# Six sweeps over one matrix: a tile on chip serves two sweeps at once, chunk order alternates, and the tiles at the diagonal are held

## The chip, the core and the metric

The kernel runs on one core of a Trainium2 chip. The metric is the device time of one launch in microseconds (us). Before the change it is 1440.37 us, the median of 3 runs (1439.02 to 1440.63).

## The reference

A residual stack of four graph layers on x (4096 nodes, 128 features) and a dense fp32 matrix adj of 4096 x 4096 (64 MiB). Cut to what matters:

```python
x = layernorm(x + inv_deg * (adj @ x + beta * x) @ K + bias)                 # layer 0
h = relu(adj @ (x @ W1) + b1); h = relu(adj @ (h @ W2) + b2)                 # layer 1, width 20
x = layernorm(x + relu(relu(adj @ (h @ W3) + b3) + x))
x = layernorm(x + (adj * dinv[:, None] * dinv[None, :]) @ (x @ W + b))       # layer 2
x = layernorm(x + adj @ x + gamma * softmax(x Wl (x Wr).T) @ x @ Wh @ Wg)    # layer 3
```

adj is multiplied six times, each time with something that depends on the whole result of the time before: x (sweep 0), three times a matrix 20 wide (sweeps 1, 2, 3), the layer-2 features (sweep 4), x again (sweep 5). The attention at the end reads no adj.

## The kernel before

Everything is laid out transposed: a sweep makes 8 chunks of 512 output columns (the 512 rows of adj that belong to them), each the sum over 32 blocks of 128 source nodes. The adj tile `tile(c, g)` is 128 x 1024 fp32, 512 KB: two source blocks (2g, 2g+1) for chunk c. 16 tiles make a chunk. SyncE streams tiles into an 8-slot ring `raw` (`wait_slot` L258, the DMA L424), held back until the consumers of the tile 8 earlier are done.

- Sweep 0 (`first_sweep`, L1094): the stationary operand is a 128 x 128 block of x, the tile moves through TensorE in plain fp32. VectorE adds up the tiles for the row sums of adj (`row_sum`, L701 to 724). While it streams, 8 of the 32 blocks of each chunk are put into lasting buffers (`kept_t`, `kept_s`, `kept_v`, `resident`).
- Sweeps 1 to 3 (`narrow_sweep`, L1127): the stationary operand is a block of h, 20 columns wide. `add` (L1136) places the products of four successive blocks in four column groups of the array, `a[32 * j:...]`. The kept blocks (8, and with `kept_l` 9) come from SBUF, so 11.5 tiles of a chunk are streamed.
- Sweeps 4 and 5 (`wide_sweep`, L1185): split fp32r arithmetic. ScalarE makes `t_hi` (L589), VectorE `t_lo` (L829), TensorE three products per block. Sweep 4 streams 14 tiles a chunk and takes the last four blocks from `resident` in plain fp32 (L1227); sweep 5 streams 16.
- Each chunk has an epilogue, done during the next chunk on fixed places of each engine's program (`hooks`, L1143): the accumulator is copied to `at` (ScalarE, L534); `epilogue_1` multiplies by a small weight (for sweeps 1 and 2 `comb`, which adds the four column groups); sweeps 0, 3 and 4 then have residual and layer norm (VectorE L748 to 808, ScalarE `xn` L559), a transposition (`epilogue_3`, L1053) and a product (`epilogue_4`, L1069); sweeps 1 and 2 have a relu (L542) and `epilogue_2` (L1045). The last step writes 512 columns of the next sweep's operand: `next_h` (L576) or `laplacian_h` (L810).

All sweeps take the chunks in the order 0 to 7 and the source blocks 0 to 31, so the operand block that is finished last is needed last. Orders are written out by hand, the same on every engine; nothing is scheduled by a planner.

Of the kernel before, what the change touches and what calls it, by code (L numbers as in the profile page):

```python
# [3 lines left out]

# [3 lines left out]
F32 = mybir.dt.float32  # L8
# [56 lines left out]
def done(stage, s, c):  # L65

    return c + (1 + NC * sum(q < s for q in STAGES[stage]))


def build(nc, adj_s, x_dram, beta_in, ident_in, comb_in, w, out):  # L70
    with ExitStack() as ctx:
# [32 lines left out]
        with ExitStack() as narrow:  # L104
            kept_v = sb("kept_v", [P, NC * CW], F32, narrow)
# [5 lines left out]
        with ExitStack() as whole:  # L111
            resident = sb("resident", [P, RB, NC * CW], F32, whole)
# [58 lines left out]
        e2, e3 = e23[:, 0:CW], e23[:, CW:PW]  # L171
        free_banks = (e0, e1)
# [1187 lines left out]
```

## Time and profile before

| | us |
|---|---|
| median of 3 runs | 1440.37 |
| the profiled execution | 1445.9 |
| its span, first to last instruction | 1444.3 |
| TensorE busy in it | 1367.3 (95%) |
| VectorE busy | 899.6 (62%) |
| ScalarE busy | 709.5 (49%) |
| HBM read | 342.65 MB |

The mean granted clock of TensorE is 0.992. Busy times of matmuls have modelled ends, so a busy TensorE need not be a TensorE at its peak: sweeps with four products side by side and sweeps with one at a time both read as busy. The profile records every plain fp32 matmul as two instructions (two passes), a split fp32r one as one.

### The profile page before, as it was taken

How to read it: one execution, taken by the hardware profiler on the slowest of the kernel's cores; microseconds unless marked ns; L12 is line 12 of the kernel's file. 1: busy time of each engine (PE TensorE's matmuls, PEld its weight loads, DVE VectorE, ACT ScalarE, POOL GpSimd, SP SyncE). 2: the span in 40 equal slices, each digit the busy share in tenths (PEclk: the TensorE clock that was granted, in tenths of full speed). 3: DMA queues.
4: the chain of work that ended last, by engine and by line, in shares of the span. 5: the costliest groups of instructions: out<-in, count | busy, mean ns of one | idle time of the engine just before them, and what ended most of it. 6: DMA issues, size and time to landing. Idle time of an engine off the chain costs nothing.

```text
span 1444.3 us, 17225 instructions
## 1 busy us (share of the span) xinstructions
PE 1367.3 (95%) x5879; PEld 798.7 (55%) x5879; DVE 899.6 (62%) x1194; ACT 709.5 (49%) x883; POOL 254.9 (18%) x167
## 2 busy tenths in 40 slices
PE   6999999888898999999999999999899999999987
PEld 2555555321222222247777778888667777767754
DVE  4676777300000013368888898888788888888885
ACT  1110011111101111257777787776787887887786
POOL 0111111000000000101010000000533333345345
PEclk9999999999999999999999999999999999999999
DMA  9866677699999999998999999997000000000000
GB/s 361 332 260 233 253 277 271 248 391 406 407 404 408 408 401 408 390 362 301 313 323 309 338 324 365 354 386 271 0 0 1 0 1 0 1 1 29 0 1 29
DMA packets 103455, 345.69 MB, mean 239 GB/s; under 512 B 11610, under 2 KB 13274, under 8 KB 103386
## 3 DMA queue, kind: packets, MB, share of 16 engines
q1 hardware_dynamic: 101136, 343.98, 63.3%
q10 hardware_dynamic: 2250, 0.82, 0.2%
q8 instruction: 41, 0.67, 0.2%
q14 instruction: 28, 0.23, 0.0%
HBM read 342.65 MB, written 2.10 MB: 239 GB/s over the span
## 4 chain that ended last, share of the span: by engine, by line
PE 75%; DMA 15%; DVE 5%; ACT 3%; issue 1%; POOL 0%; SPq 0%; DVEq 0%; ACTq 0%
DMA raw<-in_adj_s 15%; PE acc L1104 11%; PE acc L1140 9%; PE acc L1202 7%; PE acc L1197 7%; PE acc L1198 7%; PE acc L1297 6%; PE acc L1124 4%; PE acc L1227 2%; PE acc L1287 2%; PE acc L1291 2%; PE acc L1288 2%; DVE t_lo L829 2%; PE e L1252 2%; PE e L1254 2%; PE e L1253 2%
## 5 line engine op out<-in xcount | busy, mean ns | idle before, releaser
L829 DVE TENSOR_TENSOR t_lo<-raw,t_hi 128x1024 fp32r<-128x1024 f32 x240 | 292.1, 1248 | 42.4 <-ACT t_hi L589 36.9
L589 ACT ACTIVATE t_hi<-raw 128x1024 fp32r<-128x1024 f32 x240 | 251.5, 1058 | 60.4 <-PE acc L1202 58.9
L1197 PE MATMUL acc<-t_hi,st_hi 128*128 128x512 f32 x480 | 202.3, 421 | 2.9 <-DVE st_lo L734 2.9
L500 POOL TENSOR_TENSOR ring_lo<-ring,p_hi 128x1024 fp32r<-128x1024 f32 x64 | 155.6, 2430 | 220.2 <-ACT p_hi L647 220.1
L1198 PE MATMUL acc<-t_hi,st_lo 128*128 128x512 f32 x480 | 187.5, 391 | 0.0
L1140 PE MATMUL acc<-raw,h_a 128*20 128x512 f32 x736 | 161.8, 599 | 25.8 <-DMA raw<-in_adj_s 25.5
L1104 PE MATMUL acc<-raw,x 128*128 128x512 f32 x384 | 174.0, 608 | 11.2 <-DMA raw<-in_adj_s 11.2
L760 DVE TENSOR_TENSOR xs<-e,bias 128x512 f32<-128x512 f32 x8 | 5.5, 690 | 272.0 <-PE e L1020 272.0
L534 ACT ACTIVATE at<-acc 128x512 f32<-128x512 f32 x48 | 28.7, 598 | 266.4 <-PE acc L1140 181.9
L913 DVE TENSOR_TENSOR ring<-ring,e 128x1024 f32<-128x1024 f32 x128 | 154.1, 1212 | 0.7 <-PE e L1267 0.6
L1202 PE MATMUL acc<-t_lo,st_hi 128*128 128x512 f32 x480 | 149.9, 393 | 0.7 <-DVE t_lo L829 0.7
L641 ACT ACTIVATE ring<-ring 128x1024 f32<-128x1024 f32 x128 | 134.3, 1054 | 25.0 <-DVE ring L913 24.9
L472 POOL COPY x<-xn 128x512 f32<-128x512 f32 (+1 forms) x24 | 20.4, 851 | 672.6 <-ACT xn L559 672.6
L1104 PEld LDWEIGHTS acc<-raw,x 128*128 128x128 f32 x384 | 73.6, 195 | 99.0 <-issue 99.0
L1297 PE MATMUL acc<-ring,x 128*128 128x512 f32 x256 | 120.9, 595 | 0.0
L724 DVE TENSOR_TENSOR rsum<-rsum,raw 128x1024 f32<-128x1024 f32 x80 | 105.6, 1320 | 17.0 <-DMA raw<-in_adj_s 11.6
L1197 PEld LDWEIGHTS acc<-t_hi,st_hi 128*128 128x128 f32 x480 | 90.2, 188 | 31.1 <-issue 8.1
L1198 PEld LDWEIGHTS acc<-t_hi,st_lo 128*128 128x128 f32 x480 | 90.3, 188 | 24.6 <-issue 7.2
L1202 PEld LDWEIGHTS acc<-t_lo,st_hi 128*128 128x128 f32 x480 | 88.8, 188 | 23.8 <-DVE t_lo L829 5.6
L1140 PEld LDWEIGHTS acc<-raw,h_a 128*20 128x20 f32 x736 | 24.4, 98 | 130.8 <-DMA raw<-in_adj_s 100.2
L1140 PE MATMUL acc<-raw,rsum 128*20 128x512 f32 x368 | 84.0, 598 | 11.8 <-DMA raw<-in_adj_s 11.7
L891 DVE TENSOR_TENSOR peak<-e,peak 128x1024 f32<-128x1024 f32 x54 | 66.1, 1224 | 41.0 <-ACT ring L653 40.9
(189 smaller groups left out, 2062.1 us busy)
## 6 DMA issues: line engine op xcount, KB each, us to landing
raw<-in_adj_s SPq DMA_DIRECT2D x600, 512.0 KB, 6.9
resident<-in_adj_s SPq DMA_DIRECT2D x16, 512.0 KB, 7.7
raw<-in_adj_s SPq DMA_DIRECT2D x24, 256.0 KB, 7.7
kept_t<-in_adj_s SPq DMA_DIRECT2D x8, 512.0 KB, 5.8
x<-in_x SPq DMA_DIRECT2D x4, 512.0 KB, 8.4
kept_s<-in_adj_s SPq DMA_DIRECT2D x8, 256.0 KB, 6.1
kept_v<-in_adj_s SPq DMA_DIRECT2D x8, 256.0 KB, 6.5
kept_l<-in_adj_s SPq DMA_DIRECT2D x8, 256.0 KB, 9.0
```

Of the source, the lines that this page charges most:

```text
L500: nc.gpsimd.tensor_tensor(ring_lo[:, n % RING, :], slot(n), p_hi[:, m % 2, :].bitcast(F32), ALU.subtract).then_inc(pl_done, 1)
L589: nc.scalar.activation(t_hi[:, (par * wide_tiles(s) + g) % HL, :], raw[:, k, :], ACT.Copy).then_inc(hi_done, 1)
L641: nc.scalar.activation(slot(n), slot(n), ACT.Exp).then_inc(exped, 1)
L724: nc.vector.tensor_tensor(mine, mine, other, ALU.add).then_inc(sum_done, 1)
L829: nc.vector.tensor_tensor(t_lo[:, k, :], raw[:, slot_no(s, c, g), :], t_hi[:, k, :].bitcast(F32), ALU.subtract).then_inc(lo_done, 1)
L913: nc.vector.tensor_tensor(part, part, row, ALU.subtract).then_inc(subbed, 1)
L1104: i = mm(a[:, :], block_of(x0, g * GB + j), raw[:, k, j * CW:(j + 1) * CW], start=(g == 0 and j == 0), stop=False)
L1140: return mm(a[32 * j:32 * j + H, :], h[:, b * H:(b + 1) * H], moving, start=(n < 4), stop=(n >= NB - 4))
L1197: mm(a[:, :], block_of(st_hi, b), hi[:, m], start=(b == 0), stop=False)
L1198: mm(a[:, :], block_of(st_lo, b), hi[:, m], start=False, stop=False)
L1202: i = mm(a[:, :], block_of(st_hi, b), lo[:, m], start=False, stop=(b == NB - 1))
L1297: r = mm(o, block_of(x, b), slot(n)[:, u * CW:(u + 1) * CW], start=(b == 0), stop=(b == NB - 1))
```

## The change

1. **Two sweeps per tile.** In sweeps 0, 1 and 2, a tile (c, d), with d the group of 512 source nodes, is also multiplied by the next sweep's operand for d, when that is finished already: `joined(s, c, d)`, true if d stands at least AHEAD[s] = 1, 2, 2 places before c in the order of the sweep. The product goes to a bank of its own (`ahead`, the halves of `rs01`), ScalarE copies it to `sums` (`store_ahead`), and the next sweep does not use that tile: `used`. Its copy to `at` adds `sums` and moves to VectorE (`evacuate_narrow`).
2. **The order alternates.** `ORDER`: sweeps 0 and 2 take chunks 0 to 7, sweeps 1 and 3 take 7 to 0.
3. **The tiles at the diagonal are held.** For each c the 4 tiles of two d (c and c+1; 6 and 7 for chunk 7) have their own 16 KB and stay from sweep 0 to sweep 3 (chunk 1's from the start of sweep 1, `load_late`), in place of one strip for all chunks. The kept tiles come last in a chunk.
4. **What follows from it.** Ring positions are now counted by a list of items (`ITEMS`). Sweep 4 has nothing held and streams all 16 tiles, its first chunk in reverse; most of its stationary operand is made during sweep 3, a chunk at a time (`st_hi`, `st_lo` 512 columns wide). Hooks in sweep 3 are spread by `TURNED`. In sweeps 1 to 3 the first chunk waits for the epilogue of the last chunk of the sweep before (`hooks(-1)`) before its own first tile.

Tiles by chunk, in each sweep's own order of chunks (an item is one tile of 512 KB used by one chunk, held or streamed):

| sweep | items per chunk | streamed per chunk | items for two sweeps |
|---|---|---|---|
| 0 | 16 each | 12 each (chunk 1: 16), and 4 x 7 into held buffers | 0, 2, 4, 6, 8, 10, 12, 14 |
| 1 | 2, 4, 6, 8, 10, 12, 14, 16 | 0, 0, 2, 4, 6, 8, 10, 12 (and 4 late) | 0, 0, 2, 4, 6, 8, 10, 12 |
| 2 | 4, 6, 8, 10, 12, 14, 16, 16 | 0, 2, 4, 6, 8, 10, 12, 12 | 0, 0, 2, 4, 6, 8, 10, 12 |
| 3 | 4, 6, 8, 10, 12, 14, 16, 16 | 0, 2, 4, 6, 8, 10, 12, 12 | none |

```diff
+ORDER = (tuple(range(NC)), tuple(reversed(range(NC))), tuple(range(NC)), tuple(reversed(range(NC))))
+AHEAD = (1, 2, 2)
+KEPT = tuple((c, c + 1) if c + 1 < NC else (c, c - 1) for c in range(NC))
+def joined(s, c, d):
+    return s < len(AHEAD) and used(s, c, d) and ORDER[s].index(c) - ORDER[s].index(d) >= AHEAD[s]
+def used(s, c, d):
+    return s == 0 or not joined(s - 1, c, d)
...
+        ahead = [rs01[:, 0:CW], rs01[:, CW:PW]]
...
+            def evacuate_narrow(s, r):
+                ...
+                dve.wait_ge(pe_acc, s * NC + r + 1)
+                dve.wait_ge(S["mm1"], done("mm1", s, r) - 1)
+                if stored(s - 1, c):
+                    dve.wait_ge(sums_done, stored(s - 1, c))
+                    nc.vector.tensor_tensor(at[:, :], acc[r % 2], sums[:, c, :], ALU.add).then_inc(S["at"], 1)
+                else:
+                    nc.vector.tensor_copy(at[:, :], acc[r % 2]).then_inc(S["at"], 1)
...
+                for n, i in enumerate(items):
+                    ...
+                    for j in range(GB):
+                        b, k = i.d * CB + i.h * GB + j, 32 * (2 * i.h + j)
+                        m = mm(a[k:k + H, :], h[:, b * H:(b + 1) * H], t[:, j * CW:(j + 1) * CW],
+                               start=(i.d == items[0].d), stop=(i.d == items[-1].d))
+                    if i.fused:
+                        for j in range(GB):
+                            b, k = i.d * CB + i.h * GB + j, 32 * (2 * (1 - i.h) + j)
+                            m = mm(f[k:k + H, :], h_next[:, b * H:(b + 1) * H], t[:, j * CW:(j + 1) * CW],
+                                   start=(i.d == joint[0]), stop=(i.d == joint[-1]))
...
-                    if s == S5:
-                        continue
-                    if g in KEPT_AFTER and not first(c):
-                        kept = [KEPT_AFTER.index(g)]
...
-                        i = mm(a[:, :], block_of(source(s), NS * GB + j), resident_of(c, j, j + 1)[:, 0, :],
-                               start=False, stop=(j == RB - 1))
```

How the instructions move. First TensorE in sweep 0, the second half of chunk 3 and the start of chunk 4, after the change. `rs` is the bank for the products put aside, `e` a bank for epilogues, `acc` the sweep's own sum.

```order
L1256 MATMUL acc<-raw,x 128x512 x8
L1203 MATMUL e<-ident,xn 128x128 x4
L1256 MATMUL acc<-kept_t,x 128x512 x4
L1219 MATMUL e<-w,xt 128x20 x4
L1256 MATMUL acc<-kept_t,x 128x512 x4
L1256 MATMUL acc<-raw,x 128x512 x4
L1264 MATMUL rs<-raw,h_a 20x512 x4
L1283 MATMUL acc<-ident,bx 128x128 x4
L1256 MATMUL acc<-raw,x 128x512 x4
L1264 MATMUL rs<-raw,h_a 20x512 x4
```

Behind each four wide products of a joined d stand four narrow ones, a set, that were not there. Next TensorE in an early chunk of a narrow sweep. Before, all of them look like this (sweep 1):

```order
L1017 MATMUL e<-at,comb 128x512
L1140 MATMUL acc<-raw,h_a 20x512 x4
L1045 MATMUL e<-w,xt 128x20 x4
L1140 MATMUL acc<-raw,h_a 20x512 x17
L1140 MATMUL acc<-kept_l,h_a 20x512
```

Now, the end of sweep 0 and the first two chunks and a half of sweep 1:

```order
L1283 MATMUL acc<-ident,bx 128x128 x4
L1163 MATMUL e<-k,at 128x128 x4
L1165 MATMUL e<-ones_f,rsum 128x1 x4
L1203 MATMUL e<-ident,xn 128x128 x4
L1219 MATMUL e<-w,xt 128x20 x4
L1324 MATMUL acc<-kept_v,h_a 20x512 x4
L1324 MATMUL acc<-kept_s,h_a 20x512 x4
L1167 MATMUL e<-at,comb 128x512
L1324 MATMUL acc<-kept_s,h_a 20x512 x4
L1195 MATMUL e<-w,xt 128x20 x4
L1324 MATMUL acc<-raw,h_a 20x512 x2
L1329 MATMUL rs<-raw,rsum 20x512 x2
```

The whole epilogue of sweep 0's last chunk now stands in a row with no tile work between its steps, and the first chunks are a few products long. Last, VectorE in sweep 3 after the change, one chunk (here the third):

```order
L855 TENSOR_TENSOR at<-acc,sums 128x512
L882 TENSOR_TENSOR xs<-e,bias 128x512
L886 SCALAR_TENSOR_TENSOR xs<-xs,xb 128x512
L898 SCALAR_TENSOR_TENSOR xs<-xs,xb 128x512
L913 BN_STATS stats<-xs 128x6 x4
L918 BN_AGGR mv<-stats 128x2 x4
L921 TENSOR_SCALAR ve<-mv 128x4
L927 RECIPROCAL rstd<-std 128x4
L929 SCALAR_TENSOR_TENSOR nmr<-mv,rstd 128x4
L936 TENSOR_TENSOR v<-e,bias_l 128x512
L938 TENSOR_TENSOR v<-v,dinv 128x512
L843 TENSOR_TENSOR st_lo<-v,st_hi 128x512
```

The copy to `at` and the making of `st_lo` are new in this queue; before, sweep 3 had only the nine rows from `xs` to `v` there.

## Rows read from the trace of the kernel before

**Rows 1.** The page: TensorE busy tenths and HBM traffic in 40 equal slices
```profile
PE   6999999888898999999999999999899999999987
GB/s 361 332 260 233 253 277 271 248 391 406 407 404 408 408 401 408 390 362 301 313 323 309 338 324 365 354 386 271 0 0 1 0 1 0 1 1 29 0 1 29
```
**Rows 2.** Windows by stage: length, busy us by engine, clock, DMA share, GB/s
```profile
44.80:265.10 220.30, 220.30 (x702) 112.54 (x703) 162.17 (x238) 25.51 (x64) 29.53 (x21) 1.00 0.70 263
265.10:391.90 126.80, 109.60 (x611) 27.40 (x610) 3.56 (x17) 14.05 (x30) 1.23 (x2) 0.97 0.96 376
391.90:510.70 118.80, 106.98 (x592) 28.01 (x592) 0.00 (x0) 12.11 (x24) 0.00 (x0) 1.00 1.03 407
510.70:632.40 121.70, 112.52 (x662) 34.62 (x662) 35.95 (x112) 24.57 (x56) 8.63 (x14) 1.00 1.02 401
632.40:663.40 31.00, 28.42 (x114) 18.67 (x114) 30.32 (x48) 21.78 (x35) 2.18 (x2) 1.00 0.88 303
663.40:825.40 162.00, 162.00 (x673) 123.68 (x673) 137.52 (x192) 118.24 (x143) 14.79 (x14) 1.00 0.92 317
...
1011.30:1444.30 433.00, 409.16 (x1623) 287.99 (x1621) 346.60 (x406) 343.23 (x364) 184.65 (x99) 0.99 0.01 6
```
**Rows 3.** TensorE in order of time, sweeps 1 and 2: start, length, what
```profile
290.50 2.77 PE L1140 MATMUL acc<-raw,h_a 128*20 128x512 f32 x24
299.84 1.12 PE L1017 MATMUL e<-at,comb 128*128 128x512 f32 x2
300.89 1.09 PE L1140 MATMUL acc<-raw,h_a 128*20 128x512 f32 x8
301.91 1.06 PE L1045 MATMUL e<-w,xt 20*128 20x20 f32 x8
302.90 1.64 PE L1140 MATMUL acc<-raw,h_a 128*20 128x512 f32 x8
304.78 1.04 PE L1140 MATMUL acc<-raw,h_a 128*20 128x512 f32 x4 [0.24 <-DMA raw<-in_adj_s]
```
**Rows 4.** ScalarE in order of time, sweep 1: relu and the copy of h
```profile
301.00 0.68 ACT L542 ACTIVATE xt<-e,b 20x512 f32<-20x512 f32 x1 [2.14 <-PE e L1017]
303.01 0.24 ACT L576 ACTIVATE rsum<-e 128x80 f32<-128x80 f32 x1 [1.33 <-PE e L1045]
```
**Rows 5.** TensorE in order of time, chunk 0, and the last weights' user on GpSimd
```profile
27.88 9.13 PE L1104 MATMUL acc<-raw,x 128*128 128x512 f32 x16 [5.17 <-DMA raw<-in_adj_s]
39.05 1.37 POOL L467 TENSOR_TENSOR bx<-x,beta 128x512 f32<-128x512 f32 x1 [38.60 <-DMA beta<-in_beta]
```
**Rows 6.** ScalarE in order of time: ends of chunks 0 and 7 of sweep 0, the norm behind
```profile
44.81 0.60 ACT L534 ACTIVATE at<-acc 128x512 f32<-128x512 f32 x1 [12.41 <-PE acc L1124]
265.17 0.60 ACT L534 ACTIVATE at<-acc 128x512 f32<-128x512 f32 x1 [7.61 <-PE acc L1124]
272.48 1.65 ACT L559 ACTIVATE xn<-xs,nmr,rstd 128x128 f32<-128x128 f32 x4 [0.44 <-DVE nmr L807]
```
**Rows 7.** Windows of 3 us behind sweep 0: clock is third from the right
```profile
275.00:278.00 3.00, 0.81 (x5) 0.04 (x2) 0.00 (x0) 0.47 (x1) 0.62 (x1) 0.95 1.00 395
278.00:281.00 3.00, 3.00 (x8) 1.32 (x8) 0.00 (x0) 0.00 (x0) 0.00 (x0) 0.50 1.03 423
```
**Rows 8.** VectorE in order of time, sweep 3, one epilogue
```profile
544.94 0.69 DVE L760 TENSOR_TENSOR xs<-e,bias 128x512 f32<-128x512 f32 x1 [2.37 <-PE e L1020]
549.22 0.16 DVE L807 SCALAR_TENSOR_TENSOR nmr<-mv,rstd 128x4 f32<-128x4 f32 x1
```
**Rows 9.** Groups of instructions in 663.4:825.4 (sweep 4 without its first chunk)
```profile
L829 DVE TENSOR_TENSOR t_lo<-raw,t_hi 128x1024 fp32r<-128x1024 f32 x98 | 119.7, 1251 | 23.3 <-ACT t_hi L589 22.5
L1227 PE MATMUL acc<-resident,v 128*128 (+1 forms) x56 | 28.5, 590 | 0.0
```
**Rows 10.** TensorE in order of time, two tiles of sweep 4 begin
```profile
710.90 0.39 PE L1197 MATMUL acc<-t_hi,st_hi 128*128 128x512 f32 x1
712.27 0.60 PE L1029 MATMUL e<-ident,at 128*128 128x128 f32 x4
```

More of the change, by code:

```diff
@@ L423, in step @@
+            first_of_1 = min(i.seq for r in range(NC) for i in ITEMS[1, r] if not i.kept)
+            def step(s, c, par):
+                if s in FLAT:
+                    flat(s, c)
+                    return
+                for g in range(NG):
+                    wait_slot(sp, s, c, g)
                     k = slot_no(s, c, g)
-                    sp.dma_start(raw[:, k, :n], tile(c, g)[:, :n]).then_inc(raw_in[k], 16)
+                    sp.dma_start(raw[:, k, :], tile(c, group_no(s, c, g))).then_inc(raw_in[k], 16)
@@ L534, in evacuate, with store_ahead @@
                 nc.scalar.activation(at[:, :], acc[par][:, :], ACT.Copy).then_inc(S["at"], 1)
+            def store_ahead(s, r):
+                if (s, r) not in STORES:
+                    return
+                act.wait_ge(pe_acc, s * NC + r + 1)
+                if s > 0:
+                    act.wait_ge(S["at"], done("at", s, r))
+                nc.scalar.activation(sums[:, row(s, r), :], ahead[r % 2], ACT.Copy).then_inc(sums_done, 1)
             def second(s, c):
@@ L602, in step @@
-                if has_before:
-                    next_h(ps, pc)
+                early = 3 if s == S4 and first(c) else 0
+                for g in range(NG):
+                    if s == S4 and first(c) and g in S4_PREPARED:
+                        stationary_hi(S4, S4_PREPARED[g])
+                    if s == S5 and first(c) and g % 2 == 0:
+                        stationary_hi(S5, g // 2)
+                    k = slot_no(s, c, g)
+                    act.wait_ge(raw_in[k], landed(s, c, g))
+                    if not (s == S4 and first(c) and g < HL):
+                        act.wait_ge(pe_tile, tile_no(s, c, g) - (HL - 1))
+                    nc.scalar.activation(t_hi[:, g % HL, :], raw[:, k, :], ACT.Copy).then_inc(hi_done, 1)
+                    if g == 2:
+                        evacuate(ps, pc, 1 - par)
+                    if g == 4:
+                        second(ps, pc)
+                    if g == 8 - early:
+                        deviation(ps, pc)
+                    if g == 10 - early:
+                        normalise(ps, pc)
+                    if g == 12 - early:
+                        transposed(ps, pc)
```

597 lines of the change are left out of this document (326 added, 271 removed).

## The prediction

> **What bounds the kernel now.** I read the 40 slices first, then the windows by stage, then each stage in order of time. TensorE reads as 95% busy throughout, but the traffic says more: about 400 GB/s from 265 to 632 us, 230 to 320 in most other stages with tiles, none in the last 433 us [rows 1, 2]. So there are two regimes.
>
> Sweep 0 is TensorE's: seven chunks take 220.3 us, 31.5 each, without a gap, at 263 GB/s [rows 2]. Sweeps 1 to 3 take 367.3 us and are bound by the stream: 407 GB/s is 1.29 us per 512 KB tile, and 12 tiles (11.5, and half a late one) or 11.5 of them make the 15 us of a chunk. TensorE waits there a little before every tile (the last row of the group) [rows 3]. Sweep 4 is again TensorE's (162 of 162 us, 23.1 a chunk), VectorE close behind with 137.5 [rows 2]. The attention reads no tile of adj; the change leaves its instructions alone, I cost it at nothing.
>
> What a tile costs TensorE differs by a factor of four. A narrow product is recorded twice; 24 records are 12 products, and they take 2.57 us without the drain of the last (2.77 with it) [rows 3]: 0.86 us for a set of four in four column groups. A wide one takes 0.86 alone (427 ns per record).
>
> **Sweep 0.** Added: a set of four narrow products for each joined d, 7+6+...+1 = 28 sets. Nothing covers them, since TensorE is full. Floor 0.86 each; with a change to another shape and back, 1.05: a single `comb` product, worth 0.86, takes 299.84 to 300.89 [rows 3]. 28 x 1.0 = **+28**. ScalarE's and VectorE's share (copies of 0.6 us) hides beside 32 us chunks. In chunk 0 the kept tiles no longer stand ahead of streamed ones, so the hole of 5.17 us [rows 5] should close, and the slow-clock work behind it, some 2 us. Against it: the small weights are issued behind x, whose last quarter now comes six transfers later (8 us); `bx` waited for them until 38.6, and the chunk ended at 44.8 [rows 5, 6]. Bounds: -7 and +3; I take **-3**, since the queue is emptier when the weights come. Sweep 0 ends at 265.1 + 25 = 290.
>
> On the changes of shape, the Trainium skill, "TensorEngine Tiling (Array Packing)", Key Properties, says that changing the tiling mode drains TensorE. By that rule the higher price stands for each of the 28; row and rule agree, and the sum with the floor would be 4 us lower.
>
> **Sweeps 1 to 3, the stream.** It falls from 280 tile loads to 42+4, 54 and 54: 154 x 1.29 = 198 us. If the stream still set the end, 169 us would go. I think it does not, for three reasons.
>
> *Products.* Sweep 1 has 144 own and 84 joint products, 57 sets, 49 us; sweep 2 has 172+84, 64 sets, 55 us; sweep 3 172, 43 sets, 37 us. The epilogue's two steps take 1.05 + 0.99 [rows 3]: 14.4 for seven chunks in sweeps 1 and 2. So sweep 1 needs 63.4 of TensorE against 59 of stream of which 8 tiles are in the ring already; sweep 2 69.4 against 69.4, again less 8 tiles. The short chunks come first and read held tiles, so the ring is full when the long ones begin (two tiles of ring remain at the end of sweep 2 by my count). Both are TensorE's by a hair; I add 1 us for stalls.
>
> *Entries.* Before, the chunk finished last was needed last. Now the first chunk of each sweep needs it at once. Behind sweep 0 that is: accumulator to the start of `xn` 7.3, `xn` 1.65 [rows 6], transposition 0.75, copy 0.6, product 1.0, copy 0.3 = **11.8**, nothing beside it on TensorE. Behind sweeps 1 and 2: copy 0.9 on VectorE, `comb` to relu 1.2, relu to the next step 0.9, that 1.1, copy of h 0.3 [rows 3, 4] = **4.4** each.
>
> *The chain in sweep 3.* VectorE's queue is now strictly one chunk after the other. From the copy to `at`: 2.1 to the first `xs` (copy, then `epilogue_1`), 4.3 to `nmr` [rows 8], then ScalarE's norm 1.65, `st_hi` 0.75, and `st_lo` 0.8, the two steps to `v` fitting in between: 10.0 us a round, 6.6 and 8 for the first two without `st_lo`. Followed through chunk by chunk, two accumulators deep, the chunks take 1.7, 3.7, 8.9, 8.6, 11.0, 13.9, 14.7, 13.6: the last three also wait in TensorE's program for the norm and its two products. That is 76, against 61 of TensorE's work and 59 of stream. With the entry, 80.5.
>
> *The clock.* Behind sweep 0 TensorE was busy 0.8 of 3 us; then the granted clock was 0.50 (1.2 of 2.4 GHz) [rows 7]. The new entries and the early chunks of sweep 3 idle for 2 to 5 us at a time. I charge 4 us at sweep 1 (6.5 us of work at half speed, part of it waits), and 4.5 in sweep 3, where products in the chain double. The Trainium skill, "TensorE: Matmul & The Clock Gate", Part 1, calls the throttled clock the default, which activity releases; by that rule, as by the row, the idle entries are paid for again in the products behind them. With a clock that stays up the sum would be 8.5 lower.
>
> Sweep 1: 11.8 + 63.4 + 0.8 + 4 = 80. Sweep 2: 4.4 + 69.4 + 1 = 75. Sweep 3: 85. Together 240, was 367.3: **-127**.
>
> **Sweep 4.** Per chunk, the four plain products of held blocks go (8 records, at least 3.4 us) and two split tiles come. One tile is 1.37 us [rows 10], so 16 x 1.37 + 0.36 for the transposition = 22.2 against 23.1. VectorE: 119.7/98 = 1.22 per tile [rows 9]; 19.6 a chunk less 14 of them leaves 2.55, plus 16 is 22.1; stream 16 x 1.29 = 20.6. Three near-equals jostle; I take 22.7: 7 x -0.43 = **-3**. The first chunk loses eight halves of operand making on VectorE but gets the norm epilogue and two tiles more, 29.5 instead of 31: **-1.5**. Sweep 5 keeps its work: 0.
>
> **Sum.** +25 - 127 - 4.5 = -106.5. The profiled execution is 1445.9 with a span of 1444.3; the median lies 5.5 below the profiled one, and I apply the difference to the median: 1440.4 - 106.5 = 1334.
>
> **Rivals.**
>
> 1. *Everything quicker.* The clock stays up (in the attention TensorE idles in small pieces, busy 409 of 433 us, at a clock of 0.99 [rows 2]), sets cost the floor in sweep 0, weights land early: 1334 - 8.5 - 4 - 3 = 1318.
> 2. *The ring is too shallow.* Eight slots must hide a landing time that was long only because the queue was full; but when TensorE frees slots in bursts, tiles come late in the long chunks. If each of the 80 tiles of the long chunks (22, 34 and 24 in the three sweeps) costs 0.4 us, 1334 + 32 = 1366. For it: sweep 2 ends with two tiles of ring to spare. Against it: sweeps 1 to 3 before held 401 to 407 GB/s with the same ring [rows 2].
> 3. *Two banks do not mix.* The rows show four groups at once within one bank and with four moving tiles. A joint item has two products for `acc` and two for `rs`. If the two pairs run one after the other, the 84 joint items of sweeps 1 and 2 cost 0.86 more, on the engine that sets the end: 1334 + 72 = 1406.
> 4. *Slower.* The same place, without any overlap in a joint item: four products in a row are 3.44 us instead of 0.86. The 84 items cost +217, and the 28 sets of sweep 0 +72: 1623. It decides from 0.95 us per set upwards (106.5 over 112 sets). Against it: groups overlapped for different tiles and different weights; only the bank is new.
> 5. *The change does not do what it says.* The table of items and the rows of the order leave no room for that: the streamed tiles of sweeps 1 to 3 are 150 and four late ones.
>
> **Chances.** Forecast 0.63, rival 1 0.13, rival 2 0.12, rival 3 0.07, rival 4 0.04, unforeseen 0.01. The forecast's own range is 1324 to 1350: the unknown of chunk 0 (-4, +6), of the clock (-5, +10). With rivals 1 and 2 it becomes 1314 to 1368, which leaves out a little over one in ten. About 0.2% (3 us) is what a measurement tells from no change. All cases but the fourth lie far below the time before; one in a hundred is for a mixture near it. Faster 0.94, same 0.01, slower 0.05.
>
> **What would show it.** Right: sweep 0 ends near 290, each chunk about 1 us longer than the last; `acc` and `rs` narrow products start together, eight records per 0.86 us; sweeps 1 and 2 show traffic of 300 GB/s, not 407, and TensorE full in their long chunks; gaps of 11 and twice 4 us between sweeps; in sweep 3 VectorE's queue is a closed chain and TensorE waits for `at` and `xn`, with clock below 1.0; sweep 4's chunks take 22 to 23 us. Wrong: joint items of 1.7 us or more; waits for `raw` in sweeps 1 and 2 summing to more than 10 us; a clock of 0.5 through whole sweeps; a sweep 4 chunk above 23.5, which would mean that VectorE or ScalarE sets it.

## The result and the profile after

The changed kernel takes 1360.42 us (median of 4 runs, 1359.1 to 1362.38) against 1440.5 for the kernel before: a ratio of 0.9447, 95% interval 0.943 to 0.9463. The prediction was 1334 in a range of 1314 to 1368. The sign and the mechanism were right; the gain is 80 us and not 106.5.

The page of the changed kernel, TensorE and the traffic in 40 slices, and what was read:

```profile
PE   8799999998999988899999999999899999999987
GB/s 374 203 338 247 234 224 207 205 203 131 369 302 377 359 285 407 300 358 374 375 380 376 333 356 360 385 355 0 1 1 0 1 1 1 0 18 15 0 1 31
HBM read 284.98 MB, written 2.10 MB: 212 GB/s over the span
```

Against [rows 1] the long stretch at 400 GB/s has gone; between slices 11 and 17 the traffic swings from 285 to 407. The windows by stage (chunk 0; the rest of sweep 0; sweeps 1, 2, 3; the first chunk of sweep 4, its other seven; sweep 5; attention), columns as in [rows 2]:

```profile
0.00:46.30 46.30, 31.45 (x73) 14.79 (x74) 20.21 (x19) 5.18 (x5) 2.47 (x6) 0.94 0.88 335
46.30:300.10 253.80, 253.80 (x925) 114.41 (x923) 161.19 (x231) 28.43 (x70) 29.13 (x21) 1.00 0.61 232
300.10:382.40 82.30, 73.75 (x555) 26.04 (x554) 8.39 (x25) 12.73 (x29) 1.22 (x2) 0.92 0.72 269
382.40:463.20 80.80, 78.31 (x592) 24.47 (x592) 5.54 (x9) 10.18 (x22) 0.00 (x0) 1.00 0.91 351
463.20:547.50 84.30, 75.66 (x494) 28.54 (x494) 44.39 (x125) 22.93 (x53) 9.08 (x14) 0.96 0.89 338
547.50:581.70 34.20, 27.92 (x119) 19.53 (x118) 27.92 (x39) 20.69 (x26) 1.23 (x2) 1.00 0.78 281
581.70:737.70 156.00, 156.00 (x701) 128.64 (x700) 150.89 (x204) 129.54 (x156) 15.93 (x14) 1.00 0.99 375
737.70:924.60 186.90, 185.31 (x839) 150.60 (x838) 165.80 (x160) 144.03 (x156) 11.83 (x9) 1.00 0.91 343
924.60:1357.30 432.70, 409.04 (x1622) 288.13 (x1620) 345.55 (x406) 342.80 (x364) 184.38 (x99) 0.99 0.01 6
```

Sweeps 1 to 3 went from 367.3 us [rows 2] to 247.4, with the clock at 0.92 to 1.00. Sweep 0 pays 35 for it. Each stage beside its forecast:

| stage | before | forecast | after | miss |
|---|---|---|---|---|
| chunk 0 of sweep 0 | 44.8 | 41.8 | 46.3 | +4.5 |
| rest of sweep 0 | 220.3 | 248.3 | 253.8 | +5.5 |
| sweep 1 | 126.8 | 80 | 82.3 | +2.3 |
| sweep 2 | 118.8 | 75 | 80.8 | +5.8 |
| sweep 3 | 121.7 | 85 | 84.3 | -0.7 |
| sweep 4, first chunk | 31.0 | 29.5 | 34.2 | +4.7 |
| sweep 4, seven chunks | 162.0 | 159 | 156.0 | -3.0 |
| sweep 5 | 185.9 | 185.9 | 186.9 | +1.0 |

With rounding these make the 19.5 us by which the spans' difference (1444.3 - 1357.3 = 87.0) falls short of 106.5. The remaining 7 of the 106.5 - 80 lie between span and median: the profiled execution of before lay 5.5 above its median, that of the change lies 1.3 below.

The chunk lengths below are differences between the starts of the copies of `acc` to `at`, one per chunk; they repeat from kernel to kernel to 0.05 us where the stream and the clock stay out of it. So the small edits are read from them; the medians of single edits of 3 us and less hardly stand out. (Sweep 3's last chunk ends here at its copy, 551.25 us in the changed kernel; the windows above end it at the first product of sweep 4, 547.5.) Chunk s.r is the r-th that sweep s works on (r from 0). Here the lengths in sweeps 0 to 3, and under them those of kernels of the experiments:

```
            0.0   .1   .2   .3   .4   .5   .6   .7 | 1.0   .1   .2   .3   .4   .5   .6   .7
changed    46.4 33.1 33.8 35.0 36.2 37.4 38.5 39.7 |14.9  3.8  8.2  8.3  9.2 10.9 12.6 14.3
before     44.8 31.5 31.5 31.5 31.5 31.5 31.5 31.5 |20.7 12.4 15.7 15.4 15.4 15.4 15.4 16.3
no joint   45.1 32.3 31.5 31.5 31.5 31.5 31.5 31.5 |25.9 17.0 15.3 15.4 15.3 15.4 15.3 15.3
all six    36.8 32.7 33.9 34.7 35.9 36.7 37.9 38.8 |12.7  4.5  6.3  8.6  9.2 10.9 12.6 14.3

            2.0   .1   .2   .3   .4   .5   .6   .7 | 3.0   .1   .2   .3   .4   .5   .6   .7
changed     5.6  5.7  7.4  9.2 10.1 12.1 15.3 15.4 | 7.2  6.4  8.8  9.3  9.3 15.3 13.9 17.8
before     16.5 13.2 14.7 14.7 15.3 14.8 14.7 14.8 |16.5 14.9 14.9 14.9 15.5 15.1 15.2 16.8
no joint   18.9 14.1 15.4 15.4 15.4 15.4 16.2 15.4 |16.9 16.9 15.3 15.4 15.3 16.7 15.3 18.8
no joint 2  5.6  5.7  6.6  7.4  8.3 12.5 15.3 15.3 |15.9 16.3 15.4 15.3 15.3 16.7 15.4 18.8
all six     5.6  3.8  8.3  8.3 10.0 11.8 15.7 15.4 | 5.6  6.3  8.3  7.6  8.3 16.0 14.2 19.0
```

### The profile page after: what moved, and what is told of

Its sections match the earlier page's. It is cut to its first block, busy times and chain, and to the rows that moved or that the text cites. A ratio compares the mean times of both kernels' runs of the same rounds, so it can differ in the third digit from the quotient of the medians.

```text
span 1357.3 us, 17259 instructions
## 1 busy us (share of the span) xinstructions
PE 1291.2 (95%) x5911; PEld 795.1 (59%) x5911; DVE 929.9 (69%) x1213; ACT 716.5 (53%) x880; POOL 255.3 (19%) x167
## 3 DMA queue, kind: packets, MB, share of 16 engines
HBM read 284.98 MB, written 2.10 MB: 212 GB/s over the span
## 4 chain that ended last, share of the span: by engine, by line
PE 69%; DVE 13%; issue 6%; ACT 5%; DMA 3%; ACTq 1%; SPq 1%; POOL 1%; DVEq 0%; POOLq 0%
PE acc L1256 14%; PE acc L1324 8%; PE acc L1445 7%; DVE t_lo L989 7%; PE acc L1363 4%; PE acc L1358 4%; PE acc L1359 4%; DMA raw<-in_adj_s 2%; PE rs L1264 2%; PE acc L1435 2%; PE acc L1436 2%; PE acc L1439 2%; PE rs L1329 2%; PE e L1400 2%; PE e L1402 2%
## 5 line engine op out<-in xcount | busy, mean ns | idle before, releaser
L989 DVE TENSOR_TENSOR t_lo<-raw,t_hi 128x1024 fp32r<-128x1024 f32 x256 | 307.4, 1243 | 23.9 <-ACT t_hi L711 18.9
L711 ACT ACTIVATE t_hi<-raw 128x1024 fp32r<-128x1024 f32 x256 | 262.8, 1055 | 39.5 <-PE acc L1363 37.8
L1359 PE MATMUL acc<-t_hi,st_lo 128*128 128x512 f32 x512 | 199.6, 390 | 0.0
L584 POOL TENSOR_TENSOR ring_lo<-ring,p_hi 128x1024 fp32r<-128x1024 f32 x64 | 155.4, 2428 | 220.4 <-ACT p_hi L765 220.3
L1363 PE MATMUL acc<-t_lo,st_hi 128*128 128x512 f32 x512 | 159.9, 393 | 5.3 <-DVE t_lo L989 5.0
L1358 PEld LDWEIGHTS acc<-t_hi,st_hi 128*128 128x128 f32 x512 | 96.2, 188 | 25.5 <-issue 3.1
L1359 PEld LDWEIGHTS acc<-t_hi,st_lo 128*128 128x128 f32 x512 | 96.2, 188 | 19.5 <-issue 0.2
L1041 DVE TENSOR_TENSOR peak<-rs,peak 128x1024 f32<-128x1024 f32 x61 | 74.5, 1221 | 25.5 <-ACT ring L771 25.3
L855 DVE TENSOR_TENSOR at<-acc,sums 128x512 f32<-128x512 f32 x19 | 13.1, 689 | 109.4 <-PE acc L1324 109.4
L771 ACT ACTIVATE ring<-rs 128x1024 f32<-128x1024 f32 x62 | 63.3, 1021 | 37.5 <-PE rs L1402 37.4
L1324 PE MATMUL acc<-raw,h_a 128*20 128x512 f32 x384 | 80.7, 600 | 2.1 <-DMA raw<-in_adj_s 1.4
L1400 PE MATMUL e<-q_hi,k_hi 128*128 128x512 f32 x122 | 69.6, 571 | 3.6 <-DVE peak L1041 1.8
```

The source lines that it names most:

```text
L584: nc.gpsimd.tensor_tensor(ring_lo[:, n % RING, :], slot(n), p_hi[:, m % 2, :].bitcast(F32), ALU.subtract).then_inc(pl_done, 1)
L711: nc.scalar.activation(t_hi[:, g % HL, :], raw[:, k, :], ACT.Copy).then_inc(hi_done, 1)
L989: nc.vector.tensor_tensor(t_lo[:, k, :], raw[:, slot_no(s, c, g), :], t_hi[:, k, :].bitcast(F32), ALU.subtract).then_inc(lo_done, 1)
L1041: nc.vector.tensor_tensor(peak[:, :], score_bank(t)[:, :], peak[:, :], ALU.max).then_inc(s_maxed, 1)
L1324: m = mm(a[k:k + H, :], h[:, b * H:(b + 1) * H], t[:, j * CW:(j + 1) * CW], start=(i.d == items[0].d), stop=(i.d == items[-1].d))
L1358: mm(a[:, :], block_of(st_hi, b), hi[:, m], start=(g == 0 and j == 0), stop=False)
```

## The experiments

**Where the gain comes from: joint tiles off.** All edits are made to the changed kernel.

```
-AHEAD = (1, 2, 2)
+AHEAD = (99, 99, 99)
```

> Edit to the changed kernel: no tile serves two sweeps (AHEAD = 99, 99, 99); the order of chunks still alternates and the tiles at the diagonal are still the ones held. Theory (the whole gain is the tiles that are not streamed a second time; the alternating order and the other choice of held tiles are worth nothing by themselves): sweep 0 gets 33 us shorter than in the changed kernel, sweeps 1 to 3 take 120 to 126 us each, the whole 1436 to 1448 us, within 0.5% of the kernel before. Rival (the order and the held tiles bring part of the gain): below 1430.

Measured: 1464.54 us, ratio 1.0154 (1.0136 to 1.0171). Both theories fell: without the joint tiles the rest of the change is a loss of 22 us. One window holds all of sweep 2:

```profile
401.10:527.10 126.00, 111.80 (x592) 27.42 (x592) 5.54 (x8) 7.33 (x16) 0.00 (x0) 0.97 1.01 400
```

The stream is as full as before [rows 2], and the products are the same 592, but 126.0 us in place of 118.8. The new layout holds 4 tiles of a row on chip, the old one 4.5 (blocks 23 to 31), so a full row streams 12 tiles and not 11.5: a chunk in the middle of sweep 2 takes 15.36 us, before 14.74. By the copies of `acc`, sweeps 1 to 3 lose 22.2 us and sweep 0 loses 1.0, while sweep 4, which holds nothing now, wins 4.4; that is 18.8 in all, less than the medians' 22, since the profiled execution of before lay above its median. Three sweeps stream 12 tiles more; at 1.28 us each they are worth 15 of those 22.2. The excess shows most in the first two chunks of a sweep (42.9 against 33.1 in sweep 1, 33.0 against 29.8 in sweep 2), where the program now puts the epilogue of the last chunk ahead of every product: in sweep 1 TensorE waits 6.20 us for `xn`, where before it worked through 16 products of the new sweep. Alternating order and held tiles were not tried apart from each other, so how the loss divides between them is not shown. The joint tiles bring 104 us (1464.5 to 1360.4); 80 is what is left when the order and the storage that they need are paid.

**Joint tiles off in one sweep.**

```
-AHEAD = (1, 2, 2)
+AHEAD = (99, 2, 2)
```

> Edit to the changed kernel: sweep 0 no longer puts products for sweep 1 aside (AHEAD = 99, 2, 2), so that sweep 1 reads all its tiles. Theory (a set put in between full-height products costs 1.18 us, 28 of them): sweep 0 behind chunk 0 takes 221 us in place of 253.9, sweep 1 is stream-bound at 12 x 1.285 = 15.4 us per chunk, 124 to 128 us in place of 82.3, the whole 1370 to 1376. Rival (sweep 0's extra time is in part its epilogues' new waits): sweep 0 behind chunk 0 stays above 228.

Measured: 1378.29 us (2 runs; 0.9558, 0.9538 to 0.9578). Sweep 0 behind chunk 0 takes 221.6 us against 253.85: 32.25 / 28 = 1.15 us per set, and the chunks of sweep 0 in the table grow by 1.18 from one to the next. The theory holds for sweep 0. Sweep 1 took 134.6, more than I expected, because the same two first chunks cost 42.4 here; the whole lies 2 us above my range for it.

```
-AHEAD = (1, 2, 2)
+AHEAD = (1, 2, 99)
```

> Edit to the changed kernel: sweep 2 no longer puts products for sweep 3 aside (AHEAD = 1, 2, 99), so that sweep 3 reads all its tiles. Theory (21 joint sets of 0.86 us go; where a chunk is bound by the stream they cost nothing): sweep 2 goes from 80.8 to 68 to 73 us, its last two chunks stay at 15.3 us, sweep 3 from 84.3 to 124 to 128 us, the whole 1388 to 1396. Rival (sets beside the others run at no cost, since they fill column groups that stood empty): sweep 2 stays above 78, the whole above 1398.

Measured: 1396.99 us (2 runs; 0.9688, 0.9668 to 0.9707). Sweep 2 took 76.8, between theory and rival. Chunks 2.2 and 2.3, with one and two sets less, are 0.86 and 1.72 us shorter; 2.4 is 1.76 shorter for three sets; 2.5 is 0.4 longer for four less, 2.6 and 2.7 unchanged. The whole is 1 us above my range. A joint set costs TensorE 0.86 in the early chunks and nothing in the late ones, where the stream sets the time:

```profile
383.67:424.00 40.33, 38.49 (x248) 13.10 (x248) 4.15 (x6) 5.97 (x13) 0.00 (x0) 1.00 0.87 325
424.00:460.50 36.50, 33.01 (x178) 7.46 (x176) 1.39 (x3) 1.83 (x4) 0.00 (x0) 1.00 1.03 410
```

In the changed kernel the last two chunks of sweep 2 run at the same rate, VectorE's copies of `acc` 15.3 us apart, which is 12 tiles:

```profile
432.48 0.69 DVE L855 TENSOR_TENSOR at<-acc,sums 128x512 f32<-128x512 f32 x1 [11.44 <-PE acc L1324]
447.82 0.69 DVE L857 COPY at<-acc 128x512 f32<-128x512 f32 x1 [14.65 <-PE acc L1324]
463.18 0.69 DVE L857 COPY at<-acc 128x512 f32<-128x512 f32 x1 [14.66 <-PE acc L1324]
```

**Chunk 0.** In the changed kernel TensorE (first row) and GpSimd (second) end it like this:

```profile
44.27 2.05 PE L1283 MATMUL acc<-ident,bx 128*128 128x128 f32 x8 [8.73 <-POOL bx L551]
...
43.08 1.04 POOL L551 TENSOR_TENSOR bx<-x,beta 128x512 f32<-128x512 f32 x1 [42.63 <-DMA beta<-in_beta]
```

`bx` waits for `beta`, the last constant, and starts 4.0 us later than before [rows 5], and TensorE stands for 8.7 us; then its clock is down (0.64 in 38 to 46 us) and the products behind take twice their time.

```
-            act.wait_ge(x_in[XP - 1], 16)
+            act.wait_ge(x_in[0], 16)
             for dst, src in consts:
```

> Edit to the changed kernel: ScalarE starts the DMAs of the constants when the first quarter of x has landed, not the last. Theory (chunk 0 waits for these loads: beta is the last of them and GpSimd's bx waits for it, TensorE then idles 8.7 us): the end of chunk 0 goes from 46.3 to 36 to 38 us, the whole to 1350 to 1352 us (-8 to -10). Rival (the loads take the queue time that tiles of row 0 need, so the tiles come later by as much): chunk 0 ends at 44 to 47 us, the whole stays within 2 us of 1360.

Measured: 1350.7 us (0.9369, 0.9344 to 0.9395), chunk 0 in 37.6. The same two instructions:

```profile
36.50 1.05 PE L1283 MATMUL acc<-ident,bx 128*128 128x128 f32 x8
...
32.34 1.12 POOL L551 TENSOR_TENSOR bx<-x,beta 128x512 f32<-128x512 f32 x1 [31.89 <-DMA beta<-in_beta]
```

The idle time is gone and the clock stays at 1.00 (2.4 GHz). The rival was right that the tiles come later: VectorE starts its ninth addition of a ring tile at 28.55 us, 25.81 in the changed kernel. But they are not late for TensorE, whose 48 records on ring tiles take 20.76 us in both kernels, without a wait. The theory holds.

**The sets of sweep 0.** One set between full-height products, in the changed kernel:

```profile
79.28 3.60 PE L1256 MATMUL acc<-raw,x 128*128 128x512 f32 x8
82.81 1.05 PE L1264 MATMUL rs<-raw,h_a 128*20 128x512 f32 x8
83.79 1.16 PE L1163 MATMUL e<-k,at 128*128 128x128 f32 x8
```

Eight full-height records are worth 8 x 0.427 = 3.42 us, but the set begins 3.53 us after them and takes 0.98 itself, not 0.86. The edit puts off the products of every first of two neighbouring source chunks and issues both sets behind the second:

```
+at = joint.index(i.d) // 2
+odd = at % 2 == 1
+alone_set = at >= (len(joint) // 2 - 1) // 2 * 2
-for b in range(CB):
+for back in ((2, 0) if odd and not alone_set else (0,) if alone_set else ()):
+    q = items[n - back].d
+    for b in range(CB):
...
-    elif i.h == 1:
+    elif i.h == 1 and alone_set:
         m.then_inc(pe_tile, 2)
+    elif i.h == 1 and odd:
+        m.then_inc(pe_tile, 4)
```

> Edit to the changed kernel: in sweep 0 the sets put aside for sweep 1 come in pairs, two sets of four products behind every second source chunk, where the source chunks stand next to each other (9 pairs of the 28 sets); the number of products is the same. Theory (a set costs 0.86 us for its products and 0.32 for the two changes between full-height products and column groups, together the measured 1.18): chunks 3 to 7 of sweep 0 get 0.32, 0.32, 0.64, 0.64 and 0.96 us shorter, the whole 2.9 us shorter, 1356.5 to 1358.5. Rival (1.18 us is what four such products take, whatever stands beside them): no chunk changes by over 0.1 us.

Measured: 1356.16 us (0.9418, 0.9404 to 0.9432). Chunks 3 to 7 are 0.33, 0.32, 0.66, 0.65 and 0.92 us shorter. A pair of sets is 16 records, and takes 1.85 us from its start to the start of what follows:

```profile
118.58 3.68 PE L1256 MATMUL acc<-raw,x 128*128 128x512 f32 x8
122.19 1.91 PE L1269 MATMUL rs<-raw,h_a 128*20 128x512 f32 x16
124.04 1.12 PE L1256 MATMUL acc<-raw,x 128*128 128x512 f32 x2
```

The eight records ahead take 3.61 of which 3.42 is theirs, the 16 take 1.85 of which 1.72: 0.32 for the change of shape and back, and 0.86 for each four products. The whole is 4.3 us shorter by the medians, more than the 2.9 of the chunks; single executions of it spread over 4.5 us.

**Half-filled sets.** TensorE in the changed kernel where chunk 2.3 begins; every product has two records, and `rs` is the bank for the next sweep:

```profile
400.09 0.60 PE L1324 MATMUL acc<-raw,rsum 128*20 128x512 f32 x2
400.50 0.60 PE L1324 MATMUL acc<-kept_e,rsum 128*20 128x512 f32 x2
400.52 0.60 PE L1324 MATMUL acc<-raw,rsum 128*20 128x512 f32 x2
400.94 1.05 PE L1329 MATMUL rs<-raw,h_a 128*20 128x512 f32 x8
401.79 1.03 PE L1324 MATMUL acc<-raw,rsum 128*20 128x512 f32 x4
402.75 1.13 PE L1167 MATMUL e<-at,comb 128*128 128x512 f32 x2
```

The two items have eight products in all, two full sets. But the `acc` products of the first half went ahead beside the chunk before, all four `rs` products follow at 400.94, and the `acc` products of the second half run alone at 401.79, two of them in the 0.86 us of four, since a full-height product comes next. An item with its h = 0 half directly ahead of an epilogue leaves such a hole. The edit moves the second epilogue behind an h = 1 half:

```
-if ps < 3 and (n == (min(4, len(items) - 1) if r > 0 else -1)):
+if ps < 3 and (n == (min(5, len(items) - 1) if r > 0 else -1)):
```

> Edit to the changed kernel: in sweeps 1 and 2 the second epilogue product of a chunk stands behind item 5 (behind both halves of a chunk's four blocks) and not behind item 4 (between the halves). Theory (a set of four row or column groups is left half filled where another shape comes between the halves, and the two halves then take 0.86 us each): chunks 2 and 3 of sweep 1 and chunks 1 to 3 of sweep 2 get 0.8 to 1.1 us shorter each, the whole 3.5 to 5 us shorter, 1355.5 to 1357. Rival (the extra microsecond is the wait for the epilogue's operand or the switch of shape itself): the chunks keep their lengths within 0.3 us, the whole within 1 us of 1360.

Measured: 1355.06 us (0.9398, 0.9377 to 0.942). In chunks of six items the epilogue now falls into the next one, so they are read in twos: 1.2 with 1.3 takes 14.87 us, was 16.50 (-1.63); 2.1 with 2.2 takes 12.06, was 13.14 (-1.08, where a new wait for `h_a` takes 0.48 of two sets); 2.3 is 0.84 shorter. Together that is 3.55 us, or 4.0 with the wait added back: five sets at 0.81. Of the whole's 5.4 another 1.5 lies in chunk 0, where `beta` landed earlier in that run; the rest is the balance of other chunks, chunk 3.0's 1.6 less at a clock of 1.00 among them. The theory holds.

**The entry of sweep 1.** TensorE's wait, and windows with the clock third from the right:

```profile
308.99 1.11 PE L1203 MATMUL e<-ident,xn 128*128 128x128 f32 x4 [6.19 <-ACT xn L652]
```
```profile
300.00:307.00 7.00, 2.11 (x18) 1.86 (x16) 3.33 (x16) 1.46 (x4) 0.00 (x0) 0.72 0.79 293
307.00:315.00 8.00, 4.91 (x24) 3.09 (x28) 0.22 (x2) 2.48 (x6) 1.22 (x2) 0.50 0.01 6
315.00:319.00 4.00, 4.00 (x24) 0.74 (x13) 0.82 (x2) 0.68 (x1) 0.00 (x0) 0.78 0.00 0
```

```
 epilogue_1(ps, pr, pr % 2)
+pe.wait_ge(sums_done, same_bank(1, 0))
+for b in [0, 1, 2, 3, 0, 1]:
+    mm(ahead[0], h_a[:, b * 128:b * 128 + 128], kept_x[:, 0, 0:CW], start=True, stop=True)
 epilogue_3(ps, pr)
```

> Edit to the changed kernel: six full-height products into a bank that nothing reads are put on TensorE between the epilogue products of sweep 0's last chunk, in the 6 us that it idles at the entry of sweep 1. They are extra work that no output uses. Theory (the idle time lowers the granted clock, 0.60 in 300 to 315 us and 0.78 in 315 to 319, and the products behind run at half speed): the granted clock from 307 to 319 us is above 0.9 and the sweep gets 2.5 to 4 us shorter, the whole 1356 to 1358. Rival (the entry is set by the chain of ScalarE and VectorE, not by products at a low clock): the clock rises and the time changes by under 1 us.

Measured: 1356.43 us (0.9418, 0.9393 to 0.9444). The windows of that kernel:

```profile
300.60:307.00 6.40, 5.72 (x25) 3.60 (x26) 3.18 (x15) 1.26 (x3) 0.00 (x0) 1.00 0.78 275
307.00:313.40 6.40, 4.36 (x28) 2.20 (x30) 0.42 (x4) 2.69 (x7) 1.23 (x2) 1.00 0.13 53
313.40:319.00 5.60, 5.09 (x38) 1.83 (x34) 1.34 (x2) 0.92 (x2) 0.00 (x0) 1.00 0.01 3
```

Chunks 1.0 and 1.1 take 12.74 + 2.92 us in place of 14.87 + 3.81: 3.0 us less. The clock of 0.5 (1.2 GHz) cost 3 us here, and the chain through ScalarE and VectorE the rest of the entry. The Trainium skill, "TensorE: Matmul & The Clock Gate", Part 1, says that activity releases the throttle; here products that nothing reads kept the granted clock at 1.00.

**Sweep 4's first chunk.**

```
ScalarE: deviation, normalise, transposed   g = 5, 7, 9  ->  6, 8, 12; st_hi(0) 13 -> 14
VectorE: residuals, statistics, scales      g = 2, 3, 4, 6  ->  3, 4, 5, 7; laplacian(0) 13, st_lo(0) 13 -> 14
TensorE: epilogue_3, epilogue_4             g = 8, 10  ->  9, 11
```

> Edit to the changed kernel: in the first chunk of sweep 4 the epilogue steps of sweep 3's last chunk and the preparation of stationary blocks 0 stand 1 to 3 groups later on ScalarE, VectorE and TensorE. Theory (that chunk takes 34.1 us against 22.3 for a later one partly because engines stand waiting, in program order, for epilogue steps that come too early): it becomes 28 to 31 us, the whole 3 to 6 us shorter. Rival (the chunk is bound by VectorE's work, 27.4 us busy, and by the clock): within 1.5 us of 34.1, the whole the same or up to 2 us longer.

Measured: 1358.18 us (0.941, 0.9389 to 0.9431). From the copy of `acc` at its start to the next one the chunk takes 28.0 us, was 30.46. Two waits of VectorE in the changed kernel:

```profile
554.77 0.69 DVE L882 TENSOR_TENSOR xs<-e,bias 128x512 f32<-128x512 f32 x1 [1.71 <-PE e L1170]
...
575.97 0.69 DVE L843 TENSOR_TENSOR st_lo<-v,st_hi 128x512 fp32r<-128x512 f32 x1 [0.70 <-ACT st_hi L607]
```

and the first of them with the later hooks:

```profile
558.37 0.69 DVE L882 TENSOR_TENSOR xs<-e,bias 128x512 f32<-128x512 f32 x1 [0.58 <-PE e L1171]
```

Hooks that came too early cost 2.5 us of the 4.7; my 3 to 6 was too much, and the rival's 1.5 too little.

**Four edits together.**

> The four edits together: constants asked for at the first quarter of x, second epilogue behind item 5, relaxed hooks in the first chunk of sweep 4, and six products that no output uses at the entry of sweep 1. Theory (they sit in different stretches and add up: 8.8 + 4.3 + 2.5 + 3 us by the traces of the single ones): 1340 to 1344 us, 0.930 to 0.933 of the kernel before. Rival (what is won ahead of a stretch that the stream bounds is lost in it): 1346 to 1352.

Measured: 1340.44 us, ratio 0.9292 (0.9276 to 0.9307). That is 18.9 us less than the changed kernel by the spans of the traces and 20.0 by the medians, where 18.6 was expected. They add up; the rival fell.

**Less stream in sweep 3, and what bounds its chunks.**

```
+near = 1 if s == 2 and c >= 3 else AHEAD[s] if s < len(AHEAD) else 0
-return s < len(AHEAD) and used(s, c, d) and ORDER[s].index(c) - ORDER[s].index(d) >= AHEAD[s]
+return s < len(AHEAD) and used(s, c, d) and ORDER[s].index(c) - ORDER[s].index(d) >= near
...
+if s == 2 and c >= 3:
+    last = [d for d in (c + 1, c - 1, c) if d in mine]
```

> Edit to the changed kernel: in chunks 3 to 7 of sweep 2 the tiles of the chunk just before are joint too, so that sweep 3 streams 8 tiles less, all of them in its first five chunks. Theory (those chunks of sweep 3 are bound by TensorE, the last three by the stream: 34 tiles at 1.285 us less the 8 that the ring holds): sweep 3's first five chunks get up to 0.86 us shorter each, its last three stay within 1 us of 47, sweep 2 gets 1.5 to 4 us longer, the whole between 3 us shorter and 1 us longer. Rival (8 tiles less are 8 x 1.285 = 10.3 us less wherever they are saved): the whole 6 to 9 us shorter.

Measured: 1362.65 us (0.9458, 0.9445 to 0.9471), no gain. Eight tiles less did not pay: the rival fell. Chunks 2.3 and 2.4 took the 0.86 us of one set more each, the last three of sweep 3 46.5 us, 0.5 less. (Chunks 2.0 and 2.1 took 3.3 us more in this run, as in those of the early constants and of the later `st_lo`; the granted clock there was 0.70 and 0.84 in all three. It was 0.77 in chunk 2.0 with the later hooks of sweep 4 and 1.00 in the changed kernel, which has its own dip in chunk 3.0. None of these edits touches these chunks; what decides it is open.) But half of my theory fell too. Chunks 3.3 and 3.4 kept their 9.29 us with two items less each, so TensorE does not set them. VectorE in order of time in the changed kernel, from one `at` to the next:

```profile
494.25 0.77 DVE L843 TENSOR_TENSOR st_lo<-v,st_hi 128x512 fp32r<-128x512 f32 x1 [0.91 <-ACT st_hi L607]
494.94 0.68 DVE L855 TENSOR_TENSOR at<-acc,sums 128x512 f32<-128x512 f32 x1
496.87 0.69 DVE L882 TENSOR_TENSOR xs<-e,bias 128x512 f32<-128x512 f32 x1 [1.25 <-PE e L1170]
...
503.55 0.77 DVE L843 TENSOR_TENSOR st_lo<-v,st_hi 128x512 fp32r<-128x512 f32 x1 [0.91 <-ACT st_hi L607]
504.24 0.68 DVE L855 TENSOR_TENSOR at<-acc,sums 128x512 f32<-128x512 f32 x1
```

`at` follows `st_lo` without a wait: `acc` had been ready, VectorE came late. That VectorE's order of work sets the round is so far read, not shown. The next edit takes 0.91 + 0.77 out of it:

```
 evacuate_narrow(ps, pr)
 if ps == 3:
+    if r > 3:
+        stationary_lo(S4, row(3, r - 4))
     residual_1(ps, pr)
...
-    if r > 2:
-        stationary_lo(S4, row(3, r - 3))
```

> Edit to the changed kernel: in sweep 3 VectorE prepares the low part of a stationary chunk (st_lo, 0.77 us, behind a wait of 0.91 us for ScalarE's st_hi) one chunk later, right behind its copy of acc, where it waits 1.25 us for TensorE anyhow; the last one is prepared at the start of sweep 4. Theory (the chunks of 9.3 us in sweep 3 are set by VectorE's order of work, from one copy of acc to the next, and not by TensorE): the chunks at 9.31 and 9.30 us get 0.7 to 1.7 us shorter each, sweep 4's first chunk up to 0.8 us longer, the whole 1 to 3 us shorter. Rival (TensorE, busy 9.1 and 8.5 of these 9.3 us, sets them): under 0.2 us each, the whole the same or 1 us longer.

Measured: 1359.83 us (0.9437, 0.9421 to 0.9452). Chunk 3.3 takes 8.26 us, was 9.31; 3.4 takes 9.14, was 9.30, and there VectorE now waits for TensorE:

```profile
496.08 0.69 DVE L855 TENSOR_TENSOR at<-acc,sums 128x512 f32<-128x512 f32 x1 [0.56 <-PE acc L1326]
496.69 0.68 DVE L843 TENSOR_TENSOR st_lo<-v,st_hi 128x512 fp32r<-128x512 f32 x1
...
505.22 0.69 DVE L855 TENSOR_TENSOR at<-acc,sums 128x512 f32<-128x512 f32 x1 [1.42 <-PE acc L1326]
```

The theory holds for one of the two chunks, the rival for the other, and the whole moved by 0.6 us, less than a measurement tells.

**All of it.** The four edits, the pairs, the later `st_lo`, and in sweep 3:

```
-if n == (2 if q < r - 1 else 9):
+if n == (3 if q < r - 1 else 9):
-if n == (4 if q < r - 1 else 12):
+if n == (5 if q < r - 1 else 12):
```

> The four edits together (1340.4 us), and with them the paired sets of sweep 0, the later st_lo of sweep 3, and in sweep 3 the first two epilogue hooks behind items 3 and 5 in place of 2 and 4. Theory (the pairs give their 2.9 us whatever else stands; in sweep 3 the chunks of 9.3 us get to 8.3 us or below, but its last three chunks wait for the stream and take most of that back): 1335 to 1338 us. Rival (all of it adds up, as the stream starts earlier too): 1331 to 1334.

Measured: 1336.3 us (1334.12 to 1337.21), ratio 0.9264 (0.9247 to 0.9282): the fastest version, 24 us below the changed kernel. Sweeps 1 to 3 of it:

```profile
287.30:366.40 79.10, 75.86 (x566) 26.63 (x566) 8.39 (x24) 12.74 (x29) 1.22 (x2) 0.98 0.74 278
366.40:445.20 78.80, 75.47 (x592) 23.57 (x592) 5.54 (x8) 10.18 (x22) 0.00 (x0) 1.00 0.95 362
445.20:530.50 85.30, 76.14 (x504) 28.71 (x504) 48.13 (x129) 26.63 (x57) 9.38 (x14) 1.00 0.93 357
```

Chunks 3.3 and 3.4 are down to 7.6 and 8.3 us, and 3.5 to 3.7 grew by 2.1 together: they follow the stream, at 412, 407 and 406 GB/s.

## Why the prediction was right, and where it was off

*What bounds.* Right. The stream left as the bound of sweeps 1 to 3 and TensorE took its place in most chunks; the joint items cost 0.86 a set, with `acc` and `rs` side by side (chunks 2.2 and 2.3 without them). Rivals 3 and 4 fell with that, and rival 5 with the traffic (342.65 MB read before, 284.98 after: 110 tiles, the 126 of sweeps 1 to 3 less 16 more in sweep 4). Rival 1 fell with a clock below 1.00, sets at 1.18 and late weights. The waits for `raw` that the profile names for TensorE sum to 2.1 us from 300 to 551 us, where the prediction took 10 for its own sign of being wrong; before they were 37.3.

*Chunk 0, "-3": +1.5.* The bounds (-7, +3) held it. What failed was the choice between them, "since the queue is emptier when the weights come": they came 4.0 us later than before. The early constants bring the chunk to 37.6, where my lower bound put it.

*A set in sweep 0, "28 x 1.0": 1.18.* Products 0.86, as priced. I took one change of shape and back as 0.19 from a `comb` product, and then 1.0 for a set of 1.05; the pairs show 0.32. That is 5 of the 5.5 us. The Trainium skill, "TensorEngine Tiling (Array Packing)", Key Properties, says that a change of mode drains the engine; the trace agrees, and by it the cost goes with the number of changes, not of products.

*Sweep 1, 80: 82.3.* The entry's terms add up to 11.6, not 11.8; with the clock held up it takes 11.6 from the copy of `acc` to the first product of the sweep (300.62 to 312.25 us). The clock was charged with 4 us and took 3.0. Two half-filled sets (1.6) are missing from "products", which counted 57 sets as if all were full. Some 2 us of the sweep stay open.

*Sweep 2, 75: 80.8.* "Both are TensorE's by a hair" is the step that failed. Three half-filled sets are worth 2.4 (the odd hook won 1.9, net of a wait of 0.5), and the last two chunks ran with the stream, 15.35 each against 13.2 and 14.1 of TensorE's by the sum (13 and 14 sets of 0.86, and 2.04 of epilogue): 3.4 more. The stream ran at its full rate there, 409 GB/s in both, where I had counted two tiles of the ring to spare. This is rival 2 in small: two chunks of this sweep (and the tail of sweep 3), not 80 tiles.

*Sweep 3, 85: 84.3.* The total was right, the parts half so, and that they cancel is luck. The clock was charged with 4.5. It was below 1.00 in chunks 3.0 (0.76) and 3.2 (0.81), which took 7.21 and 8.84 us; in the kernel with the pairs it was 1.00 in both, and they took 5.61 and 8.33: 2.1 us. The closed chain on VectorE exists and takes 9.3 us a round, not 10.0, and sets chunk 3.3 (with 3.4 close behind it for TensorE). The last three chunks, which I gave to the norm's chain, mostly follow the stream (403, 403 and 409 GB/s): when the chunks before them got faster, they grew by 2.1 us.

*Sweep 4.* The seven chunks take 22.3 us, which is TensorE's 22.2; I had added half a microsecond for three near-equals, and it was not needed. The first chunk, "29.5", missed that hooks moved up make three engines wait for each other: 34.2, of which 2.5 were shown to be that; 2.2 stay open.

*Not priced by itself.* The ring streams 12 tiles for a full row, not 11.5. The 54 tiles of a sweep count it, but the prediction never said what it costs: nothing where TensorE sets the time, some 0.6 us in each of the five chunks that the stream sets, and without the joint tiles 15 of the 22.2 us that sweeps 1 to 3 lose.

*The reference.* 5.5 us of the difference came with the profiled execution of before. I applied the difference to the median unscaled; nothing in one profile can tell that.

## What to carry to other kernels

When a transfer is made to serve two uses, price what makes it possible by itself: the order and the storage that the joint tiles need cost 22 us here beside a gain of 104. After the bound has moved, go through the chunks one by one: in three sweeps there were four limits (TensorE, a half-filled set, VectorE's order of work, the stream again at the end), and each answered to a different edit. Write column-group products so that a whole set stands ahead of every change of shape, and put sets next to each other.

## What the runs showed of the hardware that I had not expected

Products in different column groups don't keep the order of the program among each other. In the rows at 400.09 to 401.79 the first item's `acc` products start beside products of the chunk before. The second item's `rs` products, in the groups that are free, start at 400.94 with those of the first, ahead of its own `acc` products (401.79), which stand before them in the program. Within a group the order stays in these rows. The Trainium skill, "TensorEngine Tiling (Array Packing)", Key Properties, says that tiles run their loads and products independently, and this trace agrees; what follows from it, a last set of two products in the time of four, is what the odd hook shows (0.8 us won in each of five places, the wait added back).

A change between full-height products and column groups and back takes 0.32 us, the same for one set (1.18 less 0.86) as for two in a row (0.31 to 0.33 us won by each pair, which saves one change).

Six products that no output uses, in a gap of 6.2 us, kept the granted clock at 1.00 (2.4 GHz) instead of 0.50 (1.2 GHz) and made the work behind them 3.0 us shorter.
